# A one-core graph kernel on Trainium2: the older pair's low parts moved behind the newer pair's sums in VectorE's iteration

## The chip, the core and the metric

The kernel runs on one core of one Trainium2 chip. The metric is the time of one execution on the device in microseconds (us), lower is better. The times are medians of several runs; beside them stands one profiled execution, from which all rows and durations are read.

## What is computed

There are 3327 nodes with 256 features each (x), and a dense weighted adjacency matrix (adj). The program is two layers, each with a residual sum around it:

```python
h = relu(layernorm(x));  x = x + L0(h, adj)
h = relu(layernorm(x));  x = x + L1(h, adj)
```

L0 makes two steps. In each, the features are multiplied from the left by three matrices: adj plus identity scaled by its row sums, the same scaled by its column sums, and an attention matrix from which only the largest probabilities (0.9 of the mass) are kept. The three products go through weights, are added up as Z, and L0 ends in a layernorm of Y = h + Z with gamma and beta. L1 is an attention over the edges of adj: scores of h times edge_w against themselves, a masked softmax per row, a softmax over the nodes (node_w), and the product with h times weight, plus a bias.

## The kernel before

Nodes are padded to 26 tiles of 128 rows (NT = 26), one node on each of the 128 partitions. The program is a row of blocks with their own semaphores: `phase_h` (first layernorm and projections), `layer_step` twice (the two steps of L0, with a search for the threshold of the attention: these take most of the time), `phase_mid`, and `phase_edges` (L1). Nothing of one block overlaps the next. The order of the instructions on each engine is the order in which the code is written; engines meet at semaphores only, and an engine whose next instruction must wait stands still with everything behind it.

The change is in `phase_mid`. It takes the stored products of L0 tile by tile, finishes L0 (sum, layernorm, gamma, beta, residual), applies the next layernorm and relu, and makes the operands of the edges: transposed features times edge_w, features times weight, and the node score, the first two split into a high and a low float16 part. It works in 13 pairs of tiles (NPAIR = 13). For pair p the chain is:

- SyncE loads four pieces a tile into a ring of eight (`m_tin`, L1067 to L1070). The load of tile t + 8 is issued once x1 of tile t is ready, behind the store of that x1 (L1083).
- GpSimd (POOL) makes `side_sums` of each tile (L1099 and L1102, 128x256 each). They stand behind the inverse roots of an earlier pair in its queue.
- VectorE (DVE) makes `add_up` for each tile (L1138, L1140), then `statistics` (L1145) and `moments` (L1149) of the two results y.
- POOL's `inverse_roots(i)` (L1110 to L1118) is twelve dependent small instructions on 128x4, the longest a power (L1111). It serves two pairs at once: the y of pair i and the x1 of pair i - 1, and waits for both sets of moments.
- DVE's `normalize` for each tile (L1154, L1160) makes x1 of pair i - 1 with the roots of `inverse_roots(i - 1)`, then statistics and moments of x1.
- ScalarE (ACT) makes `positive` (L1199, relu of the normalized x1), TensorE (PE) transposes it (`turn`, L1229), ACT copies it to SBUF (`columns`, L1206), PE makes `project` (L1240, L1242, L1244), ACT copies out the high parts (`high_parts`, L1211, L1212), each for both tiles of the pair. ACT takes up pair p + 1 only after the high parts of pair p. PE reuses its four banks once the low parts of the tile four before are taken (`pr_taken`).
- DVE makes `low_parts` for each tile (L1166, L1167, L1168), which wait for the high parts (`hi_ready`).

DVE's program is a loop over i from 0 to 15 (LAG = 3). Iteration i does the low parts of pair i - 3, the sums, statistics and moments of pair i, and the normalization with statistics and moments of pair i - 1. All three are there for i from 3 to 12. `inverse_roots(i)` waits for the last moments of iteration i, so its result is needed in iteration i + 1 before the normalization.

Of the kernel before, what the change touches and what calls it, by code (L numbers as in the profile page):

```python
# [1025 lines left out]
def phase_mid(nc, sem_in, psum, sb_in, env):  # L1026
# [4 lines left out]
    LAG = 3  # L1031
# [3 lines left out]
    with ExitStack() as c:  # L1035
# [24 lines left out]
        @block.sync  # L1060
        def _(sp):
            def w2d(ap):
                return ap.rearrange("(c p) n -> p c n", p=P)

            def load(t):
                u = t % RING
                sp.dma_start(tin[:, u, 0:2, :].rearrange("p a d -> p (a d)"), sx_d[t]).then_inc(t_in[u], 16)  # L1067
                sp.dma_start(tin[:, u, 2, :], xa_d[t]).then_inc(t_in[u], 16)
                sp.dma_start(tin[:, u, 3, :], zu_d[t, :, 0:D]).then_inc(t_in[u], 16)
                sp.dma_start(tin[:, u, 4, :], env["x"][:, t, :]).then_inc(t_in[u], 16)  # L1070

            load(0)
            load(1)
            sp.dma_start(gam[:], env["gamma"]).then_inc(S["norm_in"], 16)
            sp.dma_start(bet[:], env["beta"]).then_inc(S["norm_in"], 16)
            for t in range(2, RING):
                load(t)
            sp.dma_start(ew[:], w2d(env["edge_w"])).then_inc(S["weights"], 16)
            sp.dma_start(wt[:], w2d(env["weight"])).then_inc(S["weights"], 16)
            sp.dma_start(nw[:, :, 0], env["node_w"]).then_inc(S["weights"], 16)  # L1080
            for t in range(NT):
                sp.wait_ge(S["x1_ready"], t + 1)
                sp.dma_start(x1_d[:, t, :], x1[:, t % 6]).then_inc(x1_stored[t % 6], 16)  # L1083
                if t + RING < NT:
                    load(t + RING)
                if t in (6, 10, 14):
                    k = (t - 6) // 4
                    sp.dma_start(env["adj"][:, k], env["adjR"][k]).then_inc(env["adj_in"][k], 16)
            for u in range(6):
                sp.wait_ge(x1_stored[u], 16 * len(range(u, NT, 6)))  # L1090
# [39 lines left out]
        @block.vector  # L1130
        def _(dve):
            own = Own(dve, S["own_dve"])

            def add_up(t):
                u, k = t % 4, t % RING
                dve.wait_ge(t_in[k], 64 * (t // RING + 1))
                dve.wait_ge(S["sum_ready"], 2 * t + 1)
                own.link(nc.vector.scalar_tensor_tensor(out=y[:, u], in0=tin[:, k, 0], scalar=rinv[:, t:t + 1], in1=tin[:, k, 3],  # L1138
                                                        op0=ALU.mult, op1=ALU.add))
                nc.vector.scalar_tensor_tensor(out=y[:, u], in0=tin[:, k, 1], scalar=cinv[:, t:t + 1], in1=y[:, u],  # L1140
                                               op0=ALU.mult, op1=ALU.add).then_inc(S["y_ready"], 1)

            def statistics(v, m, w):
                for k in range(2):
                    own.link(nc.vector.bn_stats(stat[:, w + k], v[:, m + k]))  # L1145

            def moments(i, w):
                for k in range(2):
                    nc.vector.bn_aggr(mv[:, i % CELLS, w + k], stat[:, w + k]).then_inc(S["moments"], 1)  # L1149

            def normalize(t):
                i, k = divmod(t, 2)
                u, m, cell = t % 4, t % 6, i % CELLS
                own.link(nc.vector.scalar_tensor_tensor(out=y[:, u], in0=y[:, u], scalar=mv[:, cell, k, 0:1], in1=gam[:],  # L1154
                                                        op0=ALU.subtract, op1=ALU.mult))
                dve.wait_ge(S["sum_ready"], 2 * t + 2)
                if t >= 6:
                    dve.wait_ge(x1_stored[m], 16 * (t // 6))
                    dve.wait_ge(S["h2_ready"], t - 5)
                nc.vector.scalar_tensor_tensor(out=x1[:, m], in0=y[:, u], scalar=inv[:, cell, k:k + 1], in1=tin[:, t % RING, 4],  # L1160
                                               op0=ALU.mult, op1=ALU.add).then_inc(S["x1_ready"], 1)

            def low_parts(t):
                cols = slice(t * P, (t + 1) * P)
                dve.wait_ge(S["hi_ready"], 2 * (t + 1))
                nc.vector.tensor_tensor(htl[:, :, cols], psR[t % 4][:, 0:D].rearrange("p (c n) -> p c n", c=KC), hth[:, :, cols], ALU.subtract)  # L1166
                nc.vector.tensor_tensor(sup[:, t, D:2 * D], psR[t % 4][:, D:2 * D], sup[:, t, 0:D], ALU.subtract)  # L1167
                nc.vector.tensor_copy(natt_in[:, t:t + 1], psH[t % 4][:, D:D + 1]).then_inc(S["pr_taken"], 1)  # L1168

            dve.wait_ge(S["cell_clear"], 1)  # L1170
            for i in range(NPAIR + LAG):
                if i >= LAG:
                    for k in range(2):
                        low_parts(2 * (i - LAG) + k)
                if i < NPAIR:
                    for k in range(2):
                        add_up(2 * i + k)
                    dve.wait_ge(S["y_ready"], 2 * (i + 1))
                    statistics(y, 2 * i % 4, 0)
                    moments(i, 0)  # L1180
                if i == 1:
                    dve.wait_ge(S["norm_in"], 32)
                if 1 <= i <= NPAIR:
                    dve.wait_ge(S["roots_ready"], i)
                    for k in range(2):
                        normalize(2 * (i - 1) + k)
                    dve.wait_ge(S["x1_ready"], 2 * i)
                    statistics(x1, 2 * (i - 1) % 6, 2)
                    moments(i, 2)
# [314 lines left out]
```

## Time and profile before

| | before |
|---|---|
| median of 3 runs | 3860.06 us |
| lowest, highest | 3859.39, 3860.59 us |
| profiled execution, its own time | 3859.73 us |
| its span, first to last instruction | 3857.9 us |
| granted TensorE clock, mean | 0.888 |
| DVE busy in the span | 3538.5 us (92%) |
| ACT busy in the span | 3104.8 us (80%) |
| the stage's part: DVE's first sum to its last copy | 3151.68 to 3308.97 us |

The span is what the trace shows; the own time is the device time of the same execution. An engine's wait is written in brackets behind the first instruction after it, with the work that released it. A timeline's row has start and duration in us; two rows that follow each other on DVE overlap by up to 0.1 us, since the next one starts while the last one drains.

### The profile page before, as it was taken

How to read it: one execution, taken by the hardware profiler on the slowest of the kernel's cores; microseconds unless marked ns; L12 is line 12 of the kernel's file. 1: busy time of each engine (PE TensorE's matmuls, PEld its weight loads, DVE VectorE, ACT ScalarE, POOL GpSimd, SP SyncE). 2: the span in 40 equal slices, each digit the busy share in tenths (PEclk: the TensorE clock that was granted, in tenths of full speed). 3: DMA queues.
4: the chain of work that ended last, by engine and by line, in shares of the span. 5: the costliest groups of instructions: out<-in, count | busy, mean ns of one | idle time of the engine just before them, and what ended most of it. 6: DMA issues, size and time to landing. Idle time of an engine off the chain costs nothing. (4 is left out here: it accounts for less than half of the span.)

```text
span 3857.9 us, 41925 instructions
## 1 busy us (share of the span) xinstructions
PE 2999.0 (78%) x14148; PEld 2096.7 (54%) x14148; DVE 3538.5 (92%) x4636; ACT 3104.8 (80%) x4477; POOL 358.7 (9%) x417
## 2 busy tenths in 40 slices
PE   6568888787878776648978879797887536799999
PEld 4456667575656654314544536354453435477777
DVE  6999999999999999699999999999999958677776
ACT  6999999999999998399899999999999812233333
POOL 3000000000000000000000000000000026234443
PEclk9689888898989988879989989898998768899999
DMA  2112231222222220311111111111111035122221
GB/s 90 62 54 86 67 101 48 89 67 78 80 68 88 74 69 15 134 34 48 48 37 47 39 50 36 41 52 35 47 41 41 7 98 174 45 103 103 95 94 50
DMA packets 108904, 254.28 MB, mean 66 GB/s; under 512 B 11984, under 2 KB 47888, under 8 KB 105360
## 3 DMA queue, kind: packets, MB, share of 16 engines
q1 hardware_dynamic: 82768, 217.76, 17.5%
q10 hardware_dynamic: 25920, 33.83, 2.5%
q8 instruction: 112, 1.84, 0.2%
q14 instruction: 104, 0.85, 0.1%
HBM read 217.47 MB, written 34.08 MB: 65 GB/s over the span
## 5 line engine op out<-in xcount | busy, mean ns | idle before, releaser
L691 DVE SCALAR_TENSOR_TENSOR s_dump<-s_rows,s_mid 128x3327 bf16<-128x3327 f32 x608 | 2238.1, 3681 | 1.0 <-issue 0.6
L637 ACT ACTIVATE s_adump<-s_rows,s_mid 128x3327 int8<-128x3327 f32 x324 | 995.1, 3071 | 10.4
L643 ACT ACTIVATE s_adump<-s_rows,s_mid 128x3327 int8<-128x3327 f32 x324 | 990.8, 3058 | 0.0
L899 PE MATMUL bank<-x,s_slab 128*128 128x512 f32 x1352 | 628.7, 608 | 0.0
L876 PE MATMUL bank<-kh,qs 128*128 128x512 f16 (+1 forms) x364 | 146.5, 402 | 368.1 <-DVE s_rows L670 357.2
L899 PEld LDWEIGHTS bank<-x,s_slab 128*128 128x128 f32 x1352 | 264.8, 197 | 277.5 <-issue 265.8
L943 PE MATMUL bank<-hb,s_wT 128*128 128x256 f32 x1352 | 356.8, 409 | 70.3 <-ACT s_wT L515 70.1
L943 PE MATMUL bank<-xab,s_wT 128*128 128x256 f32 x1352 | 350.8, 404 | 71.8 <-ACT s_wT L515 71.7
L932 PE MATMUL bank<-ident,s_rows 128*128 128x128 f32 x1352 | 229.5, 297 | 192.8 <-DVE s_rows L745 191.7
L1334 ACT ACTIVATE e_wh<-bank 128x512 f16<-128x512 f32 (+1 forms) x182 | 102.4, 565 | 342.9 <-PE bank L1438 342.8
L899 PE MATMUL bank<-hb,s_slab 128*128 128x257 f32 x1352 | 354.9, 403 | 0.0
L932 PEld LDWEIGHTS bank<-ident,s_rows 128*128 128x128 f32 x1352 | 187.5, 157 | 259.3 <-DVE s_rows L745 200.0
L943 PEld LDWEIGHTS bank<-hb,s_wT 128*128 128x128 f32 x1352 | 260.9, 204 | 120.4 <-ACT s_wT L515 53.5
L943 PEld LDWEIGHTS bank<-xab,s_wT 128*128 128x128 f32 x1352 | 259.5, 202 | 115.7 <-ACT s_wT L515 44.9
L899 PEld LDWEIGHTS bank<-hb,s_slab 128*128 128x128 f32 x1352 | 272.1, 204 | 59.3 <-issue 15.8
L876 PEld LDWEIGHTS bank<-kh,qs 128*128 128x128 f16 x364 | 42.8, 118 | 453.9 <-DVE s_rows L670 418.6
L515 ACT ACTIVATE s_wT<-bank 128x512 f32<-128x512 f32 (+1 forms) x364 | 199.2, 550 | 111.4 <-PE bank L932 110.6
L1406 DVE TENSOR_TENSOR e_wl<-bank,e_wh 128x512 f16<-128x512 f32 (+1 forms) x182 | 117.8, 649 | 138.0 <-ACT e_wh L1334 137.9
L670 DVE TENSOR_SCALAR_CACHE_REDUCE s_rows<-bank 128x512 f32<-128x512 f32 (+1 forms) x364 | 232.7, 643 | 7.9 <-PE bank L877 6.5
L1302 POOL TENSOR_TENSOR e_rows<-e_rows,e_adj 128x3328 f32<-128x3328 f32 x25 | 180.8, 7234 | 294.8 <-ACT e_rows L1314 294.8
L904 PEld LDWEIGHTS bank<-hb,strip 128*128 128x128 f32 x1352 | 190.5, 197 | 13.7
L745 DVE SCALAR_TENSOR_TENSOR s_rows<-s_rows,s_mid 128x3327 f32<-128x3327 f32 x52 | 191.4, 3681 | 0.9
(176 smaller groups left out, 4797.8 us busy)
## 6 DMA issues: line engine op xcount, KB each, us to landing
s_slab<-adjT_dram SPq DMA_DIRECT2D x104, 448.0 KB, 3.9
e_adj<-adjR_dram SPq DMA_DIRECT2D x26, 1664.0 KB, 6.9
s_slab<-adjT_dram SPq DMA_DIRECT2D x104, 384.0 KB, 3.7
strip<-adjR_dram SPq DMA_DIRECT2D x52, 448.0 KB, 3.5
strip<-adjR_dram SPq DMA_DIRECT2D x52, 384.0 KB, 3.3
su_d<-s_su_out ACTq DMA_DIRECT2D x26, 256.0 KB, 2.0
zu_d<-s_zu_out ACTq DMA_DIRECT2D x26, 256.0 KB, 2.0
sx_d<-s_sx_out ACTq DMA_DIRECT2D x26, 256.0 KB, 2.0
```

The lines of the kernel that those rows point to most:

```text
L515: nc.scalar.activation(wT[:, n % 2, 0:w], bank_of("quad", n)[:, 0:w], ACT.Copy).then_inc(S["ev_done"], 1)
L637: nc.scalar.activation(adump[:], row(g, r), ACT.Sign, bias=st(mid, g, 2), accum_out=cnt[:]).then_inc(S["a_eval"], 1)
L643: nc.scalar.activation(adump[:], row(g, r), ACT.Relu, bias=st(mid, g, 2), accum_out=gap[:]).then_inc(S["a_eval"], 1)
L670: nc.vector.tensor_scalar(rows[:, home(g, r), ch * CH:ch * CH + w], psL[n % 2][:, 0:w], 1.0, None, ALU.mult, ALU.max, accum_out=mx[:, home ...
L691: nc.vector.scalar_tensor_tensor(out=dump[:], in0=row(g, r), scalar=st(mid, g, r), in1=row(g, r), op0=ALU.is_gt, op1=ALU.mult, accum_out=s ...
L745: nc.vector.scalar_tensor_tensor(out=row(g, r), in0=row(g, r), scalar=st(mid, g, r), in1=row(g, r), op0=ALU.is_gt, op1=ALU.mult, accum_out ...
L876: nc.tensor.matmul(psL[n % 2][:, 0:w], lhs, kh2[:, cols], start=True, stop=False)
L899: ins = nc.tensor.matmul(acc, slab[:, i % NSLAB, j - PIECES[p], :], s_op[:, j, 0:SN], start=False, stop=(j == NT - 1))
L904: ins = nc.tensor.matmul(psS[t % 2][:, SN + j:SN + j + 1], strip[:, i % 2, k * P:(k + 1) * P], s_op[:, 0, D:SN], start=False, stop=(j == N ...
L932: ins = nc.tensor.transpose(bank[:, k * P:(k + 1) * P], rows[:, home(g, r), j * P:(j + 1) * P], ident[:])
L943: ins = nc.tensor.matmul(psA[f % 2][:, 0:D], wT[:, n % 2, k * P:(k + 1) * P], a_op[:, j, 0:D], start=(j == 0), stop=(j == NT - 1))
L1302: nc.gpsimd.tensor_tensor(em[:, t % 3], em[:, t % 3], adj[:, t % 3], ALU.mult).then_inc(S["w_ready"], 1)
```

## The change

In DVE's loop the two calls of `low_parts` move from the start of the iteration to behind the sums, statistics and moments of y, ahead of the normalization. Nothing is added or taken away, and no wait changes its count.

```diff
             for i in range(NPAIR + LAG):
-                if i >= LAG:
-                    for k in range(2):
-                        low_parts(2 * (i - LAG) + k)
                 if i < NPAIR:
                     for k in range(2):
                         add_up(2 * i + k)
                     dve.wait_ge(S["y_ready"], 2 * (i + 1))
                     statistics(y, 2 * i % 4, 0)
                     moments(i, 0)
+                if i >= LAG:
+                    for k in range(2):
+                        low_parts(2 * (i - LAG) + k)
                 if i == 1:
                     dve.wait_ge(S["norm_in"], 32)
                 if 1 <= i <= NPAIR:
```

First place, on DVE: the start of iteration 4, behind the last moments of iteration 3. In the rows, htl, sup and natt_in are what low_parts writes, m_y is the sum y, and m_stat and m_mv are its statistics and moments. Before:

```order
L1166 TENSOR_TENSOR htl<-bank,hth 128x2x128
L1167 TENSOR_TENSOR sup<-bank,sup 128x256
L1168 COPY natt_in<-bank 128x1
L1166 TENSOR_TENSOR htl<-bank,hth 128x2x128
L1167 TENSOR_TENSOR sup<-bank,sup 128x256
L1168 COPY natt_in<-bank 128x1
L1138 SCALAR_TENSOR_TENSOR m_y<-m_tin,rinv 128x256
L1140 SCALAR_TENSOR_TENSOR m_y<-m_tin,cinv,m_y 128x256
L1138 SCALAR_TENSOR_TENSOR m_y<-m_tin,rinv 128x256
L1140 SCALAR_TENSOR_TENSOR m_y<-m_tin,cinv,m_y 128x256
L1145 BN_STATS m_stat<-m_y 128x6 x2
L1149 BN_AGGR m_mv<-m_stat 128x2 x2
```

The sums stand behind the wait for the high parts there. Second place, the same iteration in the changed kernel, from its first statistics on (the four sums stand ahead of these rows, directly behind the moments of iteration 3; m_x is x1):

```order
L1145 BN_STATS m_stat<-m_y 128x6 x2
L1149 BN_AGGR m_mv<-m_stat 128x2 x2
L1166 TENSOR_TENSOR htl<-bank,hth 128x2x128
L1167 TENSOR_TENSOR sup<-bank,sup 128x256
L1168 COPY natt_in<-bank 128x1
L1166 TENSOR_TENSOR htl<-bank,hth 128x2x128
L1167 TENSOR_TENSOR sup<-bank,sup 128x256
L1168 COPY natt_in<-bank 128x1
L1154 SCALAR_TENSOR_TENSOR m_y<-m_y,m_mv,m_gam 128x256
L1160 SCALAR_TENSOR_TENSOR m_x<-m_y,m_inv,m_tin 128x256
L1154 SCALAR_TENSOR_TENSOR m_y<-m_y,m_mv,m_gam 128x256
L1160 SCALAR_TENSOR_TENSOR m_x<-m_y,m_inv,m_tin 128x256
```

The low parts now stand between the moments of y and the normalization, which waits for POOL's roots. Iterations 0 to 2 have no low parts and iterations 13 to 15 no sums, so their order is as before; so is that of every other engine.

## Rows read from the trace of the kernel before

**Rows 1.** Waits, 3177.87 to 3285.91 us: who for whom, us, times, longest.
```profile
DVE htl L1166 <- ACT sup L1212: 17.5, 11, 2.3
...
DVE m_y L1154 <- POOL m_nmr L1118: 2.1, 4, 0.6
```

**Rows 2.** DVE's timeline, iteration 2, without low parts: start, us, what, [idle before].
```profile
3168.22 0.25 DVE L1149 BATCH_NORM_AGGREGATE m_mv<-m_stat 128x2 f32<-128x6 f32 x2
...
3169.27 0.48 DVE L1138 SCALAR_TENSOR_TENSOR m_y<-m_tin,rinv 128x256 f32<-128x256 f32 x1
...
3171.23 0.25 DVE L1149 BATCH_NORM_AGGREGATE m_mv<-m_stat 128x2 f32<-128x6 f32 x2
3173.13 0.94 DVE L1154 SCALAR_TENSOR_TENSOR m_y<-m_y,m_mv,m_gam 128x256 f32<-128x256 f32 x1 [1.65 <-POOL m_nmr L1118]
...
3177.62 0.25 DVE L1149 BATCH_NORM_AGGREGATE m_mv<-m_stat 128x2 f32<-128x6 f32 x2
```

**Rows 3.** DVE's timeline, iterations 3, 8 and 12, and the stage's last copy.
```profile
3181.98 0.42 DVE L1166 TENSOR_TENSOR htl<-bank,hth 128x256 f16<-128x256 f32 x1 [1.38 <-ACT sup L1212]
...
3233.23 0.25 DVE L1149 BATCH_NORM_AGGREGATE m_mv<-m_stat 128x2 f32<-128x6 f32 x2
3233.39 0.39 DVE L1166 TENSOR_TENSOR htl<-bank,hth 128x256 f16<-128x256 f32 x1
...
3234.82 0.47 DVE L1138 SCALAR_TENSOR_TENSOR m_y<-m_tin,rinv 128x256 f32<-128x256 f32 x1
...
3282.78 0.48 DVE L1154 SCALAR_TENSOR_TENSOR m_y<-m_y,m_mv,m_gam 128x256 f32<-128x256 f32 x1 [0.60 <-POOL m_nmr L1118]
...
3285.66 0.25 DVE L1149 BATCH_NORM_AGGREGATE m_mv<-m_stat 128x2 f32<-128x6 f32 x2
...
3308.82 0.15 DVE L1168 COPY natt_in<-bank 128x1 f32<-128x1 f32 x1
```

**Rows 4.** POOL's timeline: the power and last root instruction, iterations 2 and 8.
```profile
3169.00 1.25 POOL L1111 TENSOR_TENSOR m_inv<-m_ve,m_power 128x4 f32<-128x4 f32 x1
...
3172.85 0.24 POOL L1118 TENSOR_SCALAR m_nmr<-m_nmr 128x4 f32<-128x4 f32 x1
...
3233.87 1.04 POOL L1111 TENSOR_TENSOR m_inv<-m_ve,m_power 128x4 f32<-128x4 f32 x1
...
3238.27 0.24 POOL L1118 TENSOR_SCALAR m_nmr<-m_nmr 128x4 f32<-128x4 f32 x1
```

**Rows 5.** ACT's timeline: first positive and last high part, pairs 3, 4, 11.
```profile
3204.13 1.09 ACT L1199 ACTIVATE m_h<-m_x,m_nmr,m_inv 128x256 f32<-128x256 f32 x2 [0.96 <-POOL m_nmr L1118]
...
3212.30 0.38 ACT L1212 ACTIVATE sup<-bank 128x256 f16<-128x256 f32 x1
3216.33 1.09 ACT L1199 ACTIVATE m_h<-m_x,m_nmr,m_inv 128x256 f32<-128x256 f32 x2 [3.65 <-POOL m_nmr L1118]
...
3225.33 0.38 ACT L1212 ACTIVATE sup<-bank 128x256 f16<-128x256 f32 x1
...
3291.27 1.09 ACT L1199 ACTIVATE m_h<-m_x,m_nmr,m_inv 128x256 f32<-128x256 f32 x2
...
3297.79 0.38 ACT L1212 ACTIVATE sup<-bank 128x256 f16<-128x256 f32 x1
```

**Rows 6.** PE's timeline: transposes of pairs 3 and 4; projections of 4 and 5.
```profile
3204.78 0.93 PE L1229 MATMUL bank<-ident,m_h 128*128 128x128 f32 x4 [2.31 <-ACT m_h L1199]
...
3216.98 1.18 PE L1229 MATMUL bank<-ident,m_h 128*128 128x128 f32 x4 [5.00 <-ACT m_h L1199]
3218.24 2.04 PE L1240 MATMUL bank<-m_hT,m_ew 128*128 128x128 f32 x8
...
3222.49 1.31 PE L1240 MATMUL bank<-m_hT,m_ew 128*128 128x128 f32 x8
...
3227.26 1.13 PE L1240 MATMUL bank<-m_hT,m_ew 128*128 128x128 f32 x8
...
3229.45 1.14 PE L1240 MATMUL bank<-m_hT,m_ew 128*128 128x128 f32 x8
```

## The prediction

> **What bounds the kernel now.** The page comes first: VectorE is busy for 92% of the span (the table above). That share is an average over stages, and it says nothing of this one, so I looked up where the moved instructions stand in time (3151.68 to 3308.97 us) and read only that stage. Call E(i) the end of the last moments of iteration i. E(2) is 3177.62 + 0.25 = 3177.87 [rows 2] and E(12) is 3285.66 + 0.25 = 3285.91 [rows 3]. The ten iterations between them are those that the change reorders. They take 108.04 us, 10.8 each.
>
> The view of the waits for just this stretch shows what VectorE stands still for: 11 times for ScalarE's last high part, 17.5 us in all, and 4 times for GpSimd's roots, 2.1 us in all [rows 1]. The first of these is the wait at the head of the iteration that the change moves. The reader should see that the sums behind it need nothing of what is awaited.
>
> Then come two loops. The first is VectorE and GpSimd: the roots start at E(i) and the normalization of iteration i + 1 needs them. The second goes through ScalarE and TensorE: after the roots of E(p+1), pair p goes through relu, transposes, projection and high parts, and is wanted by the low parts of iteration p + 3. Before, what follows the low parts in that iteration (sums, statistics, normalization) all comes after this wait; so the second loop sets the time, though it spans two iterations.
>
> **The loop without low parts.** Iteration 2 has none, and shows the first loop alone. E(1) is 3168.22 + 0.25 = 3168.47. Sums, statistics and moments end at 3171.23 + 0.25 = 3171.48, 3.01 us later; VectorE is then idle until the roots come, and normalizes from 3173.13, 4.66 after E(1) [rows 2]. GpSimd's last root instruction ended at 3172.85 + 0.24 = 3173.09 [rows 4], so it is the roots that are late. From there to E(2) are 4.74 us, and the iteration is 9.40 us long.
>
> **The part that moves.** The low parts of both tiles, when nothing is waited for, take 3234.82 - 3233.39 = 1.43 us [rows 3]. The idle piece in iteration 2 was 1.65 us [rows 2]. So the low parts fit into the hole, which ends when the roots come, and cost nothing while two conditions hold: the roots are as early as in iteration 2, and the high parts have come.
>
> First condition. The changed order puts the sums directly behind E(i), as iteration 2 had them. The roots then end 4.62 us after E [rows 2, 4]. In iteration 8 of before, whose low parts were ready at once, the sums came 1.3 us after E(7) = 3233.48 and the roots ended at 3238.51, 5.03 after it [rows 3, 4]. So the sums slow GpSimd's small instructions; started with the power, they only stretch it from 1.04 to 1.25 us [rows 4]. I take 4.62 (start of the normalization 4.66), since the new order is that of iteration 2, and keep 5.06 for the range.
>
> Second condition. Call L the time from the start of relu to the end of the pair's last high part. It was 3212.68 - 3204.13 = 8.55 us for pair 3, 9.38 for pair 4 and 6.90 for pair 11 [rows 5]. The difference is TensorE's clock: one tile's projection is 3222.49 - 3218.24 = 4.25 us from start to start at the lower level (1.2 GHz) and 3229.45 - 3227.26 = 2.19 at the higher (2.4 GHz) [rows 6]. Which L will it be? Pair 3 had TensorE idle for 2.31 us before its transposes [rows 6]. With 9.40 us an iteration and some 7.2 us of work in a pair like it, 2.2 us will be idle. So I take pair 3's 8.55. The last high part of pair p is then there at E(p+1) + 4.66 + 8.55 = E(p+2) + 3.81. The second tile's low parts start there, end 1.43 / 2 = 0.72 later at 4.53, and the normalization can start at 4.66. It just fits, and ScalarE is free 0.85 us before the next pair's relu.
>
> **The sum.**
> - Iteration 3: the first tile is ready in time, the second starts at 3181.98 as before [rows 3], which is 4.11 after E(2), and ends at 4.83. The normalization starts 0.17 later than 4.66, and the iteration takes 9.57 us.
> - Iterations 4 to 11: eight times 9.40, or 75.2 us.
> - Iteration 12: GpSimd has no side sums left beside its normalization, which took 3285.91 - 3282.78 = 3.13 us instead of 4.74 [rows 3]. So 4.66 + 3.13 = 7.79 us.
> - Together 92.56 us against 108.04: 15.48 us less.
> - From E(12) on the order is the old one. The high parts of pair 10 came 5.48 us after it (3291.39, just after the next relu in [rows 5]); they will come at 13.21 - 7.79 = 5.42. The tail of 3308.97 - 3285.91 = 23.06 us [rows 3] keeps its length within 0.1 us. The edges start when the stage has ended, and shift as a whole.
>
> No instruction is added and no other queue is reordered, so there is no other term. Two things ride along at no cost. SyncE's loads of tile t + 8 are issued when x1 of tile t is ready and are read over one iteration later, so they still have most of a shorter iteration to land. TensorE's banks are released by low parts 2 to 3 us later within an iteration, but still before E(i), and the transposes that reuse them need roots that start after E(i).
>
> The profiled execution took 3859.73 us, 0.33 below the median. It would become 3859.73 - 15.5 = 3844.2, and the median 3860.06 - 15.5 = 3844.6 us, 0.40% less. About 0.2% (7.7 us) is what a measurement of this kernel can tell from no change.
>
> **A rule on the shared port.** In iteration 2 a sum that started inside the power instruction (3169.27, the power ran from 3169.00 to 3170.25) took 0.48 us [rows 2, 4], and the block of sums, statistics and moments took 3.01 us, so it was not held up. The Trainium skill says in "SBUF — State Buffer", section "Who interferes with whom", that a VectorE instruction with two SBUF inputs and a GpSimd instruction that reads SBUF exclude each other, and that the one issued second is blocked in full. By that rule the sums would stand still behind the power in each of the iterations; here the row speaks against it, and with it the sum would end at the third rival's 3852.1 us instead of 3844.6.
>
> **The rivals.**
> 1. *The fit is loose.* If L is 9.38 as for pair 4, the low parts end after the roots. An iteration P is then the high parts' place in it, 4.66 + L - P, and 0.72 and 4.74 more, which gives P = (10.12 + L) / 2 = 9.75: 0.35 more, nine times, 3.2 us. If instead the roots take 5.06, P is 9.80, 3.6 us more. With both it is 9.95, 5.0 us more. The times are 3847.8, 3848.2 and 3849.6. For it: it fits by 0.1 us only. Against it: pair 4 came after 5.00 us of idle TensorE, pair 3 after 2.31 [rows 6].
> 2. *TensorE stays at its lower level; slower than before.* Both projections at 4.25 and slower transposes (1.18 instead of 0.93 us) make L = 6.90 + 2 x 2.06 + 0.25 = 11.3. ScalarE takes the pairs in order, so pairs follow each other every 11.2 us whatever VectorE does, twelve of them from pair 0's last high part (3181.95, just ahead of the low parts at 3181.98) to pair 12's: 134.4 us, against 126.2 before (3308.97, less 0.8 for the last low parts). That is 8.2 us more, 3868.3 us. It turns from gain to loss at L = 10.6. For it: spaced evenly, each pair comes with idle time ahead of it, while before every second pair ran close behind the other. Against it: in pair 4, after 5.00 us of idle time, the clock came up within the second projection (1.31 us instead of 2.04) [rows 6].
> 3. *The power holds up the sums.* If their block waits for the power's 1.04 us, it ends at 4.05 and the low parts at 5.5; the normalization is 0.83 us late, nine times, 7.5 us: 3852.1 us. Row by row iteration 2 speaks against it.
> 4. *Better than forecast.* All waits of the stretch gone would be 17.5 + 2.1 = 19.6 us [rows 1], and a last pair at L = 6.90 gives 1.65 us more: 3838.8 us at the most. The roots keep that away, but 1 to 3 us of it can come.
>
> **How the numbers follow.** The forecast with its small deviations, rival 4 included, has 0.79 (3841 to 3847). Rival 1 has 0.13, rival 3 has 0.03, rival 2 has 0.03, and 0.02 are left for something that cancels the gain. The range is 3841 to 3850: it takes in the bounds of the roots and of L and leaves out rivals 2 and 3. Faster by over 0.2% (below 3852.3) are the forecast, rivals 1 and 4 and some of rival 3: 0.92. Within 0.2%: 0.05. Slower: 0.03, rival 2.
>
> **What would show it.** In the profile of the changed kernel, between E(2) and E(12), VectorE's waits for the high parts should be under 3 us in all instead of 17.5, and its waits for the roots 1 to 4 us. E(2) to E(12) should be 92 to 93 us, the iterations from 4 on 9.4 us each, all alike, where before they took 10.8 on average. The power should take about 1.25 us in each of them. All sums should take 0.48 us, and all normalizations up to iteration 11 the slow 0.83 to 0.94. L should be 8.55 or 6.90. The tail should stay at 23 us. The forecast is wrong if the waits for high parts stay over 6 us, if a projection at the lower level covers both tiles, if the roots take over 5 us, or if GpSimd's side sums begin to wait for loads.

## The result, and the profile after

The changed kernel takes 3844.1 us (median of 6 runs, 3841.15 to 3847.69) against 3860.23 us (6 runs, 3859.39 to 3863.07): a ratio of 0.9960, with a 95% interval from 0.9951 to 0.9970, so 0.4% faster. The forecast was 3844.6 us. The profiled execution of the changed kernel took 3846.29 us, its span was 3844.5.

First the page of the changed kernel, busy time by engine. VectorE's busy time is 2 us more than before and the span 13.4 us shorter: what went was waiting.

```profile
PE 3004.2 (78%) x14148; PEld 2102.5 (55%) x14148; DVE 3540.4 (92%) x4636; ACT 3104.4 (81%) x4477; POOL 358.5 (9%) x417
```

Next the waits of the changed kernel from E(2) = 3177.90 to E(12) = 3270.21 us: who waits for whom, us in all, times, longest.

```profile
DVE m_y L1154 <- POOL m_nmr L1118: 1.4, 7, 0.2
DVE htl L1166 <- ACT sup L1212: 0.5, 1, 0.5
```

Before, the second of these was 17.5 us in 11 times and the first 2.1 in 4 [rows 1]. Now the timeline of VectorE in iteration 4 (start, us, what, idle before it), and GpSimd's power and last root instruction in the same iteration:

```profile
3187.04 0.25 DVE L1149 BATCH_NORM_AGGREGATE m_mv<-m_stat 128x2 f32<-128x6 f32 x2
3187.21 0.45 DVE L1138 SCALAR_TENSOR_TENSOR m_y<-m_tin,rinv 128x256 f32<-128x256 f32 x1
...
3190.05 0.25 DVE L1149 BATCH_NORM_AGGREGATE m_mv<-m_stat 128x2 f32<-128x6 f32 x2
3190.22 0.39 DVE L1166 TENSOR_TENSOR htl<-bank,hth 128x256 f16<-128x256 f32 x1
...
3191.58 0.15 DVE L1168 COPY natt_in<-bank 128x1 f32<-128x1 f32 x1
3191.94 0.94 DVE L1154 SCALAR_TENSOR_TENSOR m_y<-m_y,m_mv,m_gam 128x256 f32<-128x256 f32 x1 [0.20 <-POOL m_nmr L1118]
...
3196.43 0.25 DVE L1149 BATCH_NORM_AGGREGATE m_mv<-m_stat 128x2 f32<-128x6 f32 x2
```

```profile
3187.83 1.24 POOL L1111 TENSOR_TENSOR m_inv<-m_ve,m_power 128x4 f32<-128x4 f32 x1
...
3191.67 0.23 POOL L1118 TENSOR_SCALAR m_nmr<-m_nmr 128x4 f32<-128x4 f32 x1
```

The hole of 1.65 us that stood in iteration 2 before [rows 2] now holds the low parts, and 0.20 us of it are left. The power is 1.24 us long and the roots end at 3191.90, 4.61 after E(3) = 3187.29 [rows 2, 4]. The iteration is 9.39 us long, and so, within 0.01, is each from 3 to 11.

The lines of the two kernels show the same exchange (busy us, mean ns | idle before). From E(2) to E(12) of the kernel before:

```profile
L1154 DVE SCALAR_TENSOR_TENSOR m_y<-m_y,m_mv,m_gam 128x256 f32<-128x256 f32 x20 | 13.0, 648 | 2.1 <-POOL m_nmr L1118 2.1
L1138 DVE SCALAR_TENSOR_TENSOR m_y<-m_tin,rinv 128x256 f32<-128x256 f32 x20 | 12.2, 611 | 0.0
```

From E(2) to E(12) of the changed kernel:

```profile
L1154 DVE SCALAR_TENSOR_TENSOR m_y<-m_y,m_mv,m_gam 128x256 f32<-128x256 f32 x20 | 17.6, 878 | 1.4 <-POOL m_nmr L1118 1.4
L1138 DVE SCALAR_TENSOR_TENSOR m_y<-m_tin,rinv 128x256 f32<-128x256 f32 x20 | 9.3, 465 | 0.0
```

Before, some of each were slow; now every sum is quick and nearly every normalization is slow. The tail, which is what follows E(12) up to the end of the stage's last copy, is the one thing that grew in this execution. ScalarE's timeline of pairs 10 and 12, first relu and last high part:

```profile
3267.08 1.09 ACT L1199 ACTIVATE m_h<-m_x,m_nmr,m_inv 128x256 f32<-128x256 f32 x2 [2.51 <-POOL m_nmr L1118]
...
3276.42 0.38 ACT L1212 ACTIVATE sup<-bank 128x256 f16<-128x256 f32 x1
...
3284.98 1.09 ACT L1199 ACTIVATE m_h<-m_x,m_nmr,m_inv 128x256 f32<-128x256 f32 x2 [1.41 <-POOL m_nmr L1118]
...
3293.92 0.38 ACT L1212 ACTIVATE sup<-bank 128x256 f16<-128x256 f32 x1
```

L, the time from the start of relu to the end of the pair's last high part, is 9.72 and 9.32 us there. The stage ends at 3295.16, 24.95 us behind E(12), instead of 23.06 before. So 15.7 us were won between E(2) and E(12) (108.04 to 92.31) and 1.9 were lost behind it.

### The profile page after: what moved, and what is told of

Read it like the earlier page. It is cut to its first block and busy times, and to the rows that moved or that the text cites. A ratio compares the mean times of both kernels' runs of the same rounds, so it can differ in the third digit from the quotient of the medians.

```text
span 3844.5 us, 41925 instructions
## 1 busy us (share of the span) xinstructions
PE 3004.2 (78%) x14148; PEld 2102.5 (55%) x14148; DVE 3540.4 (92%) x4636; ACT 3104.4 (81%) x4477; POOL 358.5 (9%) x417
```

## The experiments

The explanation held up to now: two loops, and the wait for the high parts stood in a place where it cost more than the same work needs elsewhere. Its rivals are that only the wait itself counts, that only getting the sums ahead counts, or that the roots alone set the iteration. A median can't tell these apart to the microsecond, since the stage itself starts anywhere from 3149.4 to 3153.2 us in the profiles shown here and the tail varies with TensorE's clock. So each run is read from E(2) to E(12) first. For the table, E(i) was read in each kernel's VectorE timeline as in the prediction; all times in us.

| kernel | E(2) to E(12) | behind E(12) | median |
|---|---|---|---|
| before | 108.04 | 23.06 | 3860.23 |
| changed | 92.31 | 24.95 | 3844.10 |
| changed, once more | 92.66 | 20.46 | 3842.09 |
| old order, LAG 4 | 96.04 | 20.83 | 3846.06 |
| new order, LAG 4 | 92.31 | 20.89 | 3842.75 |
| low parts ahead of the statistics | 94.83 | 22.63 | 3845.88 |
| one tile moved | 98.29 | 22.43 | 3849.33 |
| no beta sums | 86.96 | 22.70 | 3835.44 |
| one correction step | 85.78 | 19.41 | 3829.36 |
| one correction step, LAG 4 | 84.70 | 17.68 | 3827.60 |
| one correction step, old order | 99.58 | 20.43 | 3845.30 |

The runs of the kernel before beside rows three to six had a median of 3859.20, beside the next three 3858.91, and beside the last two 3859.13.

**The changed kernel once more.**

> The changed kernel once more, on the chip of the next three. Its six runs lay between 3841.2 and 3847.7 us, before's between 3859.4 and 3863.1. Theory: the ten reordered iterations are fixed by GpSimd's roots and take 92.3 us in every execution; what varies is the tail behind them, where pairs 10 and 12 meet TensorE's clock at either level (23.1 us forecast, 24.95 in the profile shown). So E(2) to E(12) again 92.3 +- 0.3 us, the tail anywhere from 21.5 to 25. Rival: the spread sits in the ten iterations, and E(2) to E(12) differs by over 1 us from 92.3.

The stretch took 92.66 us, 0.1 over its bound of 92.6, so the rival, over 1 us away from 92.3, is refuted. The tail of 20.46 us fell 1.0 under the 21.5 to 25 that were expected: it varies by more than was allowed for. The extra 0.3 us of the stretch have a place, iteration 5, the one wait that the forecast's first rival named. VectorE's timeline there:

```profile
3198.39 0.15 DVE L1168 COPY natt_in<-bank 128x1 f32<-128x1 f32 x1
3199.65 0.42 DVE L1166 TENSOR_TENSOR htl<-bank,hth 128x256 f16<-128x256 f32 x1 [1.12 <-ACT sup L1212]
...
3200.39 0.70 DVE L1154 SCALAR_TENSOR_TENSOR m_y<-m_y,m_mv,m_gam 128x256 f32<-128x256 f32 x1
...
3202.86 0.48 DVE L1160 SCALAR_TENSOR_TENSOR m_x<-m_y,m_inv,m_tin 128x256 f32<-128x256 f32 x1
```

Pair 2 had L = 9.54 us in this execution, and its last high part came late. The normalization began 5.57 us behind E(4) = 3194.82 instead of 4.66, 0.9 late, but the iteration was only 0.33 us longer (9.73). The first instruction of the normalization took 0.70 instead of 0.94 and the last 0.48 instead of 0.83: GpSimd's side sums had started on time and were over at 3202.55, and what began late was disturbed less. The ratio to before was 0.9958 (0.9944 to 0.9971), the same as in the first comparison.

**The older pair in the old order.** The low parts stay at the head but are never late:

```diff
-    LAG = 3
+    LAG = 4
```

> Before's order with LAG = 4: the low parts stay at the iteration's start, but are those of a pair one older, whose high parts are long there. Theory of two loops: no wait for high parts is left in the stretch, but the sums stand 1.3 us behind E again and slow the roots, 5.03 to 5.06 us instead of 4.62, so an iteration takes 9.80 instead of 9.39 and E(2) to E(12) 96 us; the tail is 1.5 to 3 us shorter than 23, since the normalization of iteration 13 no longer waits for pair 10. Median 3845 to 3847. Rival 'the wait alone': what counted was the wait for high parts and the place of the sums does not matter, then E(2) to E(12) is 92.3 as in the changed kernel and the roots take 4.6. Rival 'the place alone': the older pair does nothing, 3858 to 3861.

The stretch was 96.04 us, the ratio 0.9966 (0.9953 to 0.9978). VectorE and GpSimd in iteration 6 of this kernel:

```profile
3206.88 0.25 DVE L1149 BATCH_NORM_AGGREGATE m_mv<-m_stat 128x2 f32<-128x6 f32 x2
...
3208.48 0.47 DVE L1138 SCALAR_TENSOR_TENSOR m_y<-m_tin,rinv 128x256 f32<-128x256 f32 x1
...
3212.20 0.93 DVE L1154 SCALAR_TENSOR_TENSOR m_y<-m_y,m_mv,m_gam 128x256 f32<-128x256 f32 x1 [0.60 <-POOL m_nmr L1118]
```

```profile
3207.53 1.04 POOL L1111 TENSOR_TENSOR m_inv<-m_ve,m_power 128x4 f32<-128x4 f32 x1
...
3209.09 0.44 POOL L1114 TENSOR_TENSOR m_cor<-m_cor,m_ve 128x4 f32<-128x4 f32 x1
...
3211.93 0.23 POOL L1118 TENSOR_SCALAR m_nmr<-m_nmr 128x4 f32<-128x4 f32 x1
```

The high parts are no longer waited for, and 12.0 of the 15.7 us are there without any reordering. The power is short (1.04), but the sums fall on the small instructions behind it, which take up to 0.44 us instead of 0.20; the roots end 5.03 behind E(5) and the iteration is 9.80 us. "The wait alone" would have given 92.3 and is refuted, "the place alone" 108 as well. Taken in this order, the two parts of the gain are 12.0 us for the wait and 3.7 for the place of the sums. The tail was 20.83 us, 2.2 less than before and so as short as expected, but the next run shows that this can't be put down to the older pair.

**The older pair in the new order.**

```diff
-    LAG = 3
+    LAG = 4
```

> The changed order with LAG = 4. Theory of two loops: the high parts are not late in the changed kernel except once (0.5 us in iteration 3, hidden behind the roots), so E(2) to E(12) stays 92.3 us, and the whole difference is in the tail, 1.5 to 3 us shorter, because the normalization of iteration 13 stands behind low parts that are ready. Median 3841.3 to 3843, about 1.5 to 3 us under the changed kernel on the same chip. Rival: the high parts still hold the loop in some iterations, then E(2) to E(12) falls by over 1 us.

The stretch was 92.31 us, to the hundredth that of the changed kernel: it has nothing to gain from earlier high parts. The tail was 20.89 us, but that of the changed kernel on the same chip was 20.46, and the medians (3842.75, 3842.09) don't differ. The 1.5 to 3 us expected of the tail, and of the median, were not seen; whether they exist stays open, since two tails of the changed kernel alone differ by 4.5 us.

**One step earlier.** The low parts stand behind the sums, ahead of statistics and moments of y:

```diff
                     for k in range(2):
                         add_up(2 * i + k)
+                if i >= LAG:
+                    for k in range(2):
+                        low_parts(2 * (i - LAG) + k)
+                if i < NPAIR:
                     dve.wait_ge(S["y_ready"], 2 * (i + 1))
                     statistics(y, 2 * i % 4, 0)
                     moments(i, 0)
-                if i >= LAG:
-                    for k in range(2):
-                        low_parts(2 * (i - LAG) + k)
```

> The changed kernel with the low parts one step earlier: behind the sums, ahead of the statistics of y. Nothing else moves and VectorE's work is the same. Theory of two loops: the second tile's high parts come 3.2 to 3.8 us after E, the low parts end 0.72 later, and statistics and moments (1.07) now stand behind them, so the normalization starts at 4.9 to 5.0 instead of 4.66. An iteration is (11.19 + L) / 2 = 9.7 us with L = 8.2, E(2) to E(12) 95 us, waits for high parts 5 to 9 us in the stretch, waits for roots near 0. About 3 us over the changed kernel. Rival 'the sums first is enough': getting the sums ahead of the wait is the whole effect, then it is within 0.5 us of the changed kernel.

Its waits in the stretch:

```profile
DVE htl L1166 <- ACT sup L1213: 8.4, 8, 1.6
...
DVE m_y L1154 <- POOL m_nmr L1118: 1.2, 4, 0.3
```

The stretch was 94.83 us, with iterations of 9.39 where the pair's L was 6.9 and 9.73 to 9.98 where it was longer. 8.4 us of waits cost 2.5 us, because 1.65 us of each iteration were a hole anyway. The median was 3.8 us over that of the changed kernel on the same chip (expected: about 3), so "the sums first is enough" (within 0.5) is refuted. The sums ahead of the wait are most of the effect, not the whole.

**One tile moved.** The first tile's low parts stay at the head, the second tile's stand behind the moments:

```diff
             for i in range(NPAIR + LAG):
+                if i >= LAG:
+                    low_parts(2 * (i - LAG))
                 if i < NPAIR:
...
                 if i >= LAG:
-                    for k in range(2):
-                        low_parts(2 * (i - LAG) + k)
+                    low_parts(2 * (i - LAG) + 1)
```

> Half of the change: the first tile's low parts stay at the iteration's head, the second tile's stand behind the moments. Theory of two loops: the first tile's high parts come 2.2 us before the second's, 1.1 to 1.6 us after E, so VectorE waits that long at the head again, and sums, statistics and moments (3.01) and the second low parts (0.72) follow. The normalization starts near 5.9, an iteration is (11.65 + L) / 2 = 9.9 us with L = 8.2, E(2) to E(12) 97 us, 4.5 to 5 us over the changed kernel: 3846 to 3848. Rival 'half the wait, half the gain': E(2) to E(12) halfway between 108 and 92.3, 100 us. Rival 'the second tile is the wait': within 1 us of the changed kernel.

VectorE waited for high parts 11.4 us (8 times), and the stretch was 98.29 us, the ratio 0.9973 (0.9963 to 0.9983). That is 1.3 us over the theory's number and 1.7 under the halfway mark, so it doesn't refute "half the wait, half the gain" by itself. The median of 3849.33 lies 1.3 us over the 3846 to 3848 that were expected, and the stretch is 6.0 us over that of the changed kernel instead of 4.5 to 5. Only "the second tile is the wait" (within 1 us) is refuted. The working had left a term out: with the first tile at the head, the sums stand 0.7 us or more behind E again, and the roots took 4.9 to 5.15 us in eight of the ten iterations.

**No beta sums.** One of GpSimd's two side sums per tile is gone, and beta with it:

```diff
-                nc.gpsimd.tensor_tensor(tin[:, u, 3], tin[:, u, 3], tin[:, u, 2], ALU.add).then_inc(S["sum_ready"], 1)
-                if t == 0:
-                    pool.wait_ge(S["norm_in"], 32)
-                nc.gpsimd.tensor_tensor(tin[:, u, 4], tin[:, u, 4], bet[:], ALU.add).then_inc(S["sum_ready"], 1)
+                nc.gpsimd.tensor_tensor(tin[:, u, 3], tin[:, u, 3], tin[:, u, 2], ALU.add).then_inc(S["sum_ready"], 2)
```

> The changed kernel without the second of GpSimd's two side sums per tile (L1102: x + beta is left out, so beta is missing from the output). Theory: what bounds an iteration now is roots (4.61) plus a normalization that GpSimd's side sums stretch from 3.1 to 4.74 us. With half of the side sums it is stretched over half its length only, about 3.9 us; an iteration is then 8.6 to 8.8 us (the high parts become late again at 8.8), E(2) to E(12) 85 to 87 us, 5 to 7 us under the changed kernel. Rival: the side sums have nothing to do with it, iterations stay at 9.39.

VectorE's normalization in iteration 8 of this kernel, and its end:

```profile
3223.80 0.93 DVE L1151 SCALAR_TENSOR_TENSOR m_y<-m_y,m_mv,m_gam 128x256 f32<-128x256 f32 x1 [0.20 <-POOL m_nmr L1115]
3224.77 0.83 DVE L1157 SCALAR_TENSOR_TENSOR m_x<-m_y,m_inv,m_tin 128x256 f32<-128x256 f32 x1
3225.53 0.47 DVE L1151 SCALAR_TENSOR_TENSOR m_y<-m_y,m_mv,m_gam 128x256 f32<-128x256 f32 x1
...
3227.48 0.25 DVE L1146 BATCH_NORM_AGGREGATE m_mv<-m_stat 128x2 f32<-128x6 f32 x2
```

The first two instructions are slow, beside the side sums; the last two are quick. From the start to the last moments it takes 3.93 us instead of 4.74, and the iterations where the high parts are in time take 8.57 or 8.58, the others 8.63 to 9.51 (iteration 12, without side sums, 7.78). The stretch was 86.96 us and the ratio 0.9939 (0.9926 to 0.9953). So the side sums are what stretches the normalization, and half of them costs 0.8 us an iteration.

**One correction step.** Four small instructions less in the roots of each pair (only in this stage):

```diff
-                for _ in range(2):
+                for _ in range(1):
                     own.link(nc.gpsimd.tensor_tensor(w, r, r, ALU.mult))
```

> The changed kernel with one correction step of the inverse roots in the stage instead of two (four small GpSimd instructions less per pair; the roots are then a little less exact). The roots take 4.61 - 1.12 = 3.5 us. Theory: the low parts fill the hole, so faster roots find VectorE busy until 4.4 after E, and only 0.25 us an iteration is won there; besides, the side sums start 1.1 us earlier and leave the normalization's end undisturbed, 0.3 to 0.6 us more. An iteration of 8.6 to 9.0 us, E(2) to E(12) 85 to 89 us, 3 to 7 us under the changed kernel. Rival 'the roots alone set the iteration': 9.39 - 1.12 = 8.27 us, E(2) to E(12) 81 us.

VectorE in iteration 7 of this kernel, and the end of GpSimd's roots in it:

```profile
3212.14 0.45 DVE L1138 SCALAR_TENSOR_TENSOR m_y<-m_tin,rinv 128x256 f32<-128x256 f32 x1
...
3216.52 0.15 DVE L1168 COPY natt_in<-bank 128x1 f32<-128x1 f32 x1
3216.58 0.80 DVE L1154 SCALAR_TENSOR_TENSOR m_y<-m_y,m_mv,m_gam 128x256 f32<-128x256 f32 x1
...
3219.15 0.48 DVE L1160 SCALAR_TENSOR_TENSOR m_x<-m_y,m_inv,m_tin 128x256 f32<-128x256 f32 x1
...
3220.59 0.25 DVE L1149 BATCH_NORM_AGGREGATE m_mv<-m_stat 128x2 f32<-128x6 f32 x2
```

```profile
3215.49 0.23 POOL L1118 TENSOR_SCALAR m_nmr<-m_nmr 128x4 f32<-128x4 f32 x1
```

The roots are ready at 3215.72, while VectorE is busy with the low parts until 3216.58. No idle time is shown in this iteration: VectorE itself is now the bound, at 8.62 us. The stretch was 85.78 us and the ratio 0.9927 (0.9914 to 0.9939). 1.12 us less in the roots gave 0.77 an iteration: the normalization starts 0.29 earlier (4.36 behind E) and takes 4.26 us instead of 4.74, since the side sums end earlier, so "the roots alone set the iteration" (8.27) is refuted.

**One correction step and LAG 4.** Both edits shown above together.

> The changed order, one correction step, LAG = 4. With one step alone E(2) to E(12) was 85.8 us: iterations of 8.62 in which VectorE never waits, and three longer ones in which high parts were late (1.9 us). Theory: the pair one older takes those away, E(2) to E(12) becomes 9.4 - 1.1 = 8.3 for iteration 3 (no low parts), eight times 8.62 and 7.5, or 84.8 us, and the tail stays near 19. Median within 1.5 us of the one-step kernel: 3828 to 3831. Rival: spread of the stage's start and of TensorE's clock in the tail (2 us each in the looks so far) covers any difference.

The stretch was 84.70 us, as expected, and 0.5 us of waits were left in it. The tail was 17.68 us instead of near 19; TensorE's granted clock was 1.00 in it, and 0.95 in the one-step kernel's 19.41. The median is 3827.60 us, 0.4 under the expected range, and the ratio 0.9919 (0.9906 to 0.9933). Its interval overlaps that of the one-step kernel with LAG 3, which had 3829.36 in another comparison, so the rival that the spread covers the difference in the median stands. This is the fastest version of the study, 0.8% under the kernel before, at the price of slightly less exact roots.

**One correction step in the old order.**

> Before's order with one correction step. Theory of two loops: in the old order the loop that binds spans two iterations and holds the roots once, so 1.12 us less in the roots is won once per two iterations, 0.56 an iteration: E(2) to E(12) 108.0 - 5.6 = 102.4 us, and 1 to 2 us more in the tail, median 3851 to 3853. In the changed order the same edit gave 6.5 us in the stretch. Rival 'the roots are not on its path' (before's trace shows only 2.1 us of waits for them): no change, 3859. Rival 'once per iteration': 97 us, 3847.

The stretch was 99.58 us and the median 3845.30 (0.9965; 0.9952 to 0.9977). 8.5 us were won, between "once per two iterations" (5.6) and "once per iteration" (11). Neither number was right, and "not on its path" is refuted. The timelines show what was missing: from E(3) to E(11), two iterations took 20.2 us instead of 21.9, 1.7 less. Of these 1.1 are the roots, and 0.1 is L (8.80 instead of 8.89 on average). The time from a late high part to E, which holds the sums, was 7.25 to 7.66 us instead of 7.77 to 8.27: with shorter roots the side sums end earlier and stretch the sums less. That this is the rest of the difference is read from the rows and was not tried by itself.

## Why the prediction was right

**The bound and the moved wait.** The waits for high parts fell from 17.5 to 0.5 us (forecast: under 3), those for the roots from 2.1 to 1.4 (1 to 4). Iteration 2 was the right model for the new ones: 9.39 us against 9.40. The two LAG 4 kernels show the two loops apart: without any wait for high parts the old order needs 9.80 us an iteration, the new one 9.39.

**The roots.** 4.61 us in the changed kernel (forecast 4.62), 5.02 to 5.03 in the LAG 4 kernel in the old order, where the sums stand 1.3 us behind E.

**The third rival, the power that holds up the sums,** did not come. The sums took 0.45 to 0.48 us and the block of 3187.21 to 3190.30 was as long as in iteration 2. The power grew by 0.2 us instead, as before [rows 4].

**L.** The forecast took 8.55 us for every pair and named 6.90 as the other value. Measured were 8.09, 8.39, 8.55 and 6.89 for pairs 2 to 5, and 8.08, 8.36, 8.55 and 6.89 for pairs 6 to 9. None of these held up a normalization; the low parts of pairs 4 and 8 waited 0.1 us for them, inside the hole. In the second execution pair 2 had 9.54, as in the first rival.

**Iteration 3** was forecast at 9.57 and took 9.39. The second tile did come late, and the normalization started 0.3 us later than elsewhere. But the side sums had not waited for it, and it was disturbed for a shorter time: its first instruction took 0.62 us instead of 0.94. In the second execution 0.9 us late cost 0.33. So the first rival's price for late high parts (3.2 us) was too high, since it charged every late start in full. Its price for roots of 5.06 us was right: the kernel with roots of 5.03 us took 9.80 an iteration.

**Iteration 12** took 7.78 us instead of 7.79.

**The tail** is the term that was off. It was forecast to keep its 23.06 us within 0.1. It was 24.95 in the profiled execution and 20.46 in the other. It holds three pairs in a row, each with its own L (8.61, 6.90 and 8.55 us before; 9.72, 6.90 and 9.32 in the one, 6.89, 8.55 and 6.89 in the other). The lengths go with TensorE's granted clock behind E(12): 0.89 for 23.06 us, 0.78 for 24.95, 0.92 for 20.46. The order of work was as said; the length was one draw out of several. The sum came out at 92.31 + 24.95 = 117.26 us against 131.10, so 13.8 us less in the first profile and 18.0 in the second, around the forecast 15.5. That the medians came within 0.5 us of the forecast is luck to that extent: what was foreseen is the 15.7 us of the stretch.

**The second rival, TensorE at its lower level throughout,** did not come. Pairs came at even distances, and the clock rose within the first projection or at its end in most of them.

## What to carry to other kernels

A wait for a slow side chain belongs into a hole that another wait makes anyway, directly ahead of that wait, with all the work that needs neither of the two in front of both; the size of the hole, read from an iteration without the moved work, says in advance how much fits. A loop that spans two iterations is best found by following one item through the engines, not from the totals of waits: 17.5 us of waits for the high parts and 2.1 for the roots said little of how either would respond. When two engines disturb each other, look at what the new order puts side by side, since here 3.7 of 15.7 us came from where the sums fall on GpSimd's instructions.

## What the runs showed of the hardware

VectorE's sums and normalizations (two inputs in SBUF, 128x256) take 0.45 to 0.49 us alone and 0.83 to 0.95 beside GpSimd's side sums of the same size, while the low parts, with one input in PSUM, take 0.39 to 0.43 in either company (0.41 and 0.42 beside a side sum in the kernel with one correction step). The Trainium skill, "SBUF — State Buffer", section "SBUF: two separate sides", says that such pairs exclude each other for a whole instruction. The rows agree that they hold each other up, but not for that long. GpSimd's side sums in iteration 4 of the changed kernel, beside the normalization, whose four instructions start at 3191.94, 3192.91, 3193.66 and 3194.64 on VectorE:

```profile
3192.55 0.91 POOL L1102 TENSOR_TENSOR m_tin<-m_tin,m_bet 128x256 f32<-128x256 f32 x1
3193.42 0.90 POOL L1099 TENSOR_TENSOR m_tin<-m_tin 128x256 f32<-128x256 f32 x1
3194.28 0.90 POOL L1102 TENSOR_TENSOR m_tin<-m_tin,m_bet 128x256 f32<-128x256 f32 x1
```

One of each passes in 0.87 to 0.90 us from start to start. Apart they take 0.48 (the sums) and 0.68 us (side sums beside low parts, in the kernel with one correction step), 1.16 together. And the power instruction of 1.04 us held nothing up: it was itself stretched to 1.24, and the sum that started inside it took 0.48 us.

TensorE's clock was not expected to make a cycle. With a pair every 9.39 us, the idle time ahead of the transposes was 3.91, 2.65, 2.37 and 2.20 us, and then 3.85 again. From the timeline of TensorE in the changed kernel (transposes, and the first group of the projection behind them):

```profile
3201.98 1.05 PE L1229 MATMUL bank<-ident,m_h 128*128 128x128 f32 x4 [2.65 <-ACT m_h L1199]
3202.98 2.04 PE L1240 MATMUL bank<-m_hT,m_ew 128*128 128x128 f32 x8
...
3211.38 0.93 PE L1229 MATMUL bank<-ident,m_h 128*128 128x128 f32 x4 [2.37 <-ACT m_h L1199]
3212.38 1.57 PE L1240 MATMUL bank<-m_hT,m_ew 128*128 128x128 f32 x8
...
3220.77 0.93 PE L1229 MATMUL bank<-ident,m_h 128*128 128x128 f32 x4 [2.20 <-ACT m_h L1199]
3221.77 1.13 PE L1240 MATMUL bank<-m_hT,m_ew 128*128 128x128 f32 x8
```

Behind 2.20 us of idle time the projection ran at the higher level from its start (1.13 us), behind 2.37 it fell to the lower level within its first group (1.57), and behind 2.65 the whole group was at the lower (2.04). The idle time alone doesn't decide it, though. In the LAG 4 kernel in the old order, pairs 8 and 9 had the same (the transposes, and the second group of the first tile's projection):

```profile
3252.08 0.93 PE L1229 MATMUL bank<-ident,m_h 128*128 128x128 f32 x4 [2.62 <-ACT m_h L1199]
...
3254.05 1.89 PE L1242 MATMUL bank<-m_wt,m_hT 128*128 128x256 f32 x4
...
3261.89 0.93 PE L1229 MATMUL bank<-ident,m_h 128*128 128x128 f32 x4 [2.62 <-ACT m_h L1199]
...
3263.86 1.03 PE L1242 MATMUL bank<-m_wt,m_hT 128*128 128x256 f32 x4
```

The first fell to the lower level and had L = 8.55 us, the second stayed at the higher and had 6.89. Nor does it decide when the clock comes back: in the changed kernel pair 2 had 3.91 us of idle time and L = 8.09, pair 10 had 3.86 and L = 9.72. So the level can't be read off the idle time in advance, it is worth 1.2 to 2.8 us of L, and where no hole hides that, as in the tail, it is in the time.
